# Gated delta rule: the triangular solve of a unit split over two pipeline steps, in straight code

## The reference

```python
q = l2norm(short_conv(h @ Wq)) * SCALE; k = l2norm(short_conv(h @ Wk)); v = short_conv(h @ Wv)   # conv of 4 taps, silu
g_eff = -exp(A_log) * softplus(h @ Wf1 @ Wf2 + dt_bias)      # 8 groups of 16 key channels
beta = sigmoid(h @ Wb)
def step(S, inp):
    qt, kt, vt, gt, bt = inp
    S = S * exp(gt)[..., None]
    err = einsum('bhk,bhkv->bhv', kt, S)
    delta = bt[..., None] * (vt - err)
    S = S + kt[..., None] * delta[:, :, None, :]
    return S, einsum('bhk,bhkv->bhv', qt, S)
y = o * silu(h @ Wg + bg)
y = y * rsqrt(mean(y * y, -1) + EPS) * norm_w
return y.reshape(B, T, H * DV) @ Wo
```

## Time and profile before

| | us |
|---|---|
| median of 3 runs | 6659.9 |
| profiled execution, its own time | 6661.47 |
| its span | 6659.7 |
| TensorE busy / weight loads | 6146.7 / 4309.7 |
| VectorE busy | 4830.9 |
| ScalarE busy | 2724.6 |
| GpSimd busy | 1811.1 |

### The profile page before, as it was taken

The page is one execution under the profiler, slowest core; times in us unless marked ns, Lnnn a source line. Parts: engine busy times, 40 slices in busy tenths (PEclk is TensorE's granted clock), DMA queues, the critical chain, the costliest instruction groups (busy, mean ns, idle before and its releaser), DMA issues. The chain is left out here.

```text
span 6659.7 us, 108024 instructions
## 1 busy us (share of the span) xinstructions
PE 6146.7 (92%) x33720; PEld 4309.7 (65%) x33720; DVE 4830.9 (73%) x7947; ACT 2724.6 (41%) x4746; POOL 1811.1 (27%) x1636
## 2 busy tenths in 40 slices
PE   5699999999999999999999999999999999899999
PEld 2467766766667667766777667766777777644444
DVE  7688878888788878887888788878888888611110
ACT  2344444444444444444444444444444444401101
POOL 2233333333333333333333333333333333200000
PEclk8899999999999999999999999999999999999999
DMA  2101010100010100101010101010100000032221
GB/s 71 43 25 30 21 33 26 32 25 27 26 32 26 27 25 25 32 25 30 22 33 25 33 25 29 22 33 26 32 26 27 25 26 26 16 114 81 85 78 43
DMA packets 183592, 234.20 MB, mean 35 GB/s; under 512 B 25048, under 2 KB 128088, under 8 KB 179168
## 3 DMA queue, kind: packets, MB, share of 16 engines
q1 hardware_dynamic: 111072, 188.22, 9.7%
q10 hardware_dynamic: 72192, 41.95, 2.2%
HBM read 183.75 MB, written 46.38 MB: 35 GB/s over the span
## 5 line engine op out<-in xcount | busy, mean ns | idle before, releaser
L659 PE MATMUL bank<-xT,weights 128*128 (+1 forms) x4096 | 2183.2, 631 | 87.3 <-DMA bg_col<-in_L_attn_bg 34.6
L1185 POOL TENSOR_TENSOR KR<-KR,decay_u 128x256 f32<-128x256 f32 x896 | 979.0, 1093 | 2358.1 <-PE bank L685 2358.1
L911 DVE TENSOR_TENSOR KQ<-KQ,decay_u 128x512 f32<-128x512 f32 x896 | 759.8, 848 | 602.2 <-PE bank L685 602.0
L685 PEld LDWEIGHTS bank<-KQ,KR 128*128 128x128 f32 x7168 | 919.2, 192 | 249.7 <-issue 216.3
L896 DVE SCALAR_TENSOR_TENSOR conv<-pre,taps,conv 128x512 f32<-128x512 f32 x1152 | 993.4, 862 | 27.3
L685 PE MATMUL bank<-KQ,KR 128*128 128x128 f32 x7168 | 954.7, 276 | 1.7 <-DVE KQ L911 1.7
L659 PEld LDWEIGHTS bank<-xT,weights 128*128 128x128 f32 x4096 | 660.6, 194 | 299.4 <-issue 216.8
L931 DVE COPY_PREDICATED all_pairs<-level_mask,bank 128x512 f32<-128x512 int32 x896 | 793.4, 885 | 0.0
L707 PEld LDWEIGHTS bank<-T_inv,pairs 128*128 128x128 f32 x3072 | 457.3, 193 | 470.3 <-issue 248.3
L707 PE MATMUL bank<-T_inv,pairs 128*128 128x64 f32 x3072 | 656.0, 339 | 62.0 <-DVE T_inv L947 59.6
L1103 ACT ACTIVATE T_inv<-bank 128x256 fp32r<-128x256 f32 x640 | 248.0, 388 | 792.6 <-PE bank L722 792.6
(11 more groups left out here) (162 smaller groups left out, 9129.5 us busy)
## 6 DMA issues: line engine op xcount, KB each, us to landing
decay_u<-decay_scratch SPq DMA_DIRECT2D x128, 510.0 KB
beta_u<-beta_scratch SPq DMA_DIRECT2D x128, 256.0 KB
y_scratch<-y_out ACTq DMA_DIRECT2D x128, 256.0 KB, 6.9
y_in<-y_scratch SPq DMA_DIRECT2D x32, 1024.0 KB, 4.8
xt<-in_L_attn_hidden_states SPq DMA_DIRECT2D x8, 1024.0 KB, 5.5
x_in<-in_L_attn_hidden_states SPq DMA_DIRECT2D x32, 256.0 KB, 5.0
out<-o_out ACTq DMA_DIRECT2D x32, 256.0 KB, 2.0
w<-in_L_ffn_W SPq DMA_DIRECT2D x8, 704.0 KB, 4.9
```

What stands on the lines that cost most here:

```text
L659: last = nc.tensor.matmul(bank[w % 2][:], weights[par][:, w, k, :], xT[:, k, bass.ds(j * UC, UC)], start=k == 0, stop=k == KC - 1)
L685: last = nc.tensor.matmul(to[:, :, i], KR[:, cols(i)], halves(KQ[:, :, cols(i)], l, 1), start=True, stop=True)
L911: nc.vector.tensor_tensor(second_halves, second_halves, pair[:, :, 0:1].unsqueeze(1).to_broadcast([P, 2, blocks, 1 << l]), ALU.mult).then_ ...
L1185: nc.gpsimd.tensor_tensor(first_halves, first_halves, second.to_broadcast([P, UC >> (l + 1), 1 << l]), ALU.mult).then_inc(keys_scaled.sem, 1)
```

## The change

- A fourth role: unit `c = a - 3`. The step of `b` ends with the first delta and the product of `refine(b, 0)`; both corrections, the second refinement, output and state, the gated output, its norm and the store are done for `c` in the next step, between the projections and the first levels. X, gate, k_rows, pairs_scan and chunk_decay have two buffers each. k_hat and q_hat now lie in silu, v_u in conv, y_out in y_rn, residual in U_r.
- Banks: T goes to bank 5 and X to bank 2 in the inverse; the solve has bank 7.
- v comes into bank 7 by four transposes (`is_transpose=True`), followed by the four products with the state; before, four fp32 products with the identity alternated with them.
- ScalarE's list: the copy KQ_scan (`keep_scaled`) now stands ahead of the table load and the two `inverse_norm`; the silu of the gate is followed by the copies of T and X, projection 0 comes behind them. GpSimd makes the first X after level 2 of the step before its use.
- `walk` and SP's list are Python loops: 131 steps written out, no hardware loop. DVE no longer waits ahead of y_out for the store; ScalarE does, ahead of the Ln.

```diff
+        for n in range(H * J + 3):
+            a, m, b, c = (u if 0 <= u < H * J else None for u in (n, n - 1, n - 2, n - 3))
...
+            step(Step(**f))
@@ SP
+        for u in range(1, H * J):
+            h, j = u // J, u % J
+            if j == 1 and 1 <= h < H - 1:
+                load_next(h, h % 2)
+            wait(sp, unit_ready, u - 1, 1)
+            if u >= 2:
+                wait(sp, keys_scaled, u - 2, LEVELS)
+                wait(sp, chunk_decay_ready, u - 2, 1)
+            load_unit(h, j, u % 2)
@@ TensorE
+            def right_side():
...
                 for i in range(B):
-                    nc.tensor.matmul(bank[7][:, cols(i)], v_u[:, cols(i)], ident[:], start=True, stop=False)
+                    nc.tensor.matmul(bank[7][:, cols(i)], v_u[:, cols(i)], ident[:], is_transpose=True, start=i == 0,
+                                     stop=False, skip_group_check=True)
+                for i in range(B):
                     last = nc.tensor.matmul(bank[7][:, cols(i)], KQ_scan[:, 0, cols(i)], state[:, cols(i)], start=False,
-                                            stop=True)
+                                            stop=True, skip_group_check=True)
...
+            def y_sums():
+                if c is None:
+                    return
                 if a is not None:
                     wait(pe, sums_taken, a, 2)
+                wait(pe, y_sq_ready, c, 1)
...
+            correct_by_residual(0)
+            project(0, (0, 1))
+            inverse_z(1)
+            diagonal()
+            level(0)
+            inverse_xt(1)
+            refine(c, 1)
+            project(0, (2,))
+            inverse_z(2)
+            project(0, (3,))
+            level(1)
+            inverse_xt(2)
+            correct_by_residual(1)
+            project(1, (0,))
+            inverse_z(3)
+            project(1, (1,))
+            level(2)
+            inverse_xt(3)
+            project(1, (2,))
+            output_and_state()
+            inverse_z(4)
+            project(1, (3,))
+            level(3)
+            inverse_xt(4)
+            project(2, (0,))
+            inverse_z(5)
+            project(2, (1,))
+            level(4)
+            inverse_xt(5)
+            project(2, (2,))
+            inverse_z(6)
+            right_side()
+            level(5)
+            inverse_xt(6)
+            project(2, (3,))
+            output_of_state()
+            first_delta()
+            sums(0)
+            project(3, (0,))
+            level(6)
+            refine(b, 0)
+            sums(1)
+            project(3, (1,))
+            transpose_keys()
+            project(3, (2,))
             transpose_pairs()
+            y_sums()
+            project(3, (3,))
@@ VectorE
             halo(a, s.a_first, m, qk_conv_steps, 2 * TAPS, slice(0, 2), qk_halo_ready)
             halo(m, s.m_first, b, v_conv_steps, TAPS, slice(2, 3), v_halo_ready)
+            correct_delta(0)
             add_identity_to_z(1)
             keep_diagonal()
             scale(0)
             keep_pairs(0)
+            take_residual(c, 1)
+            add_identity_to_z(2)
+            scale(1)
+            keep_pairs(1)
+            correct_delta(1)
+            add_identity_to_z(3)
+            scale(2)
+            keep_pairs(2)
+            convolve(0, range(2))
+            gated_output()
+            add_identity_to_z(4)
+            scale(3)
+            keep_pairs(3)
+            next_state()
+            convolve(0, range(2, TAPS))
+            add_identity_to_z(5)
+            scale(4)
+            keep_pairs(4)
+            convolve(1, range(2))
+            add_identity_to_z(6)
+            scale(5)
+            keep_pairs(5)
+            convolve(1, range(2, TAPS))
             scale(LEVELS - 1)
             keep_pairs(LEVELS - 1)
+            take_residual(b, 0)
+            convolve(2)
+            keep_chunk_decay()
             unit_inputs()
             first_inverse()
+            normalised_output()
@@ ScalarE
+            silu_gate()
+            take_t(1)
+            take_x(1)
+            silu_v()
+            take_projection(0)
+            take_t(2)
+            take_x(2)
+            take_t(3)
+            take_x(3)
+            take_projection(1)
+            take_t(4)
+            take_x(4)
+            square_output()
+            silu_squares(0)
+            take_t(5)
+            take_x(5)
+            take_right_side()
+            take_x(6)
+            take_projection(2)
+            take_delta()
+            silu_squares(1)
+            keep_scaled()
+            nc.scalar.preload_act_table_set("natural_log_exp_and_others")
+            inverse_norm(0)
+            inverse_norm(1)
+            keep_rows()
+            keep_all_pairs()
+            inverse_rms()
+            store_output()
@@ GpSimd
+        def first_x(u, before):
+            wait_apart(pool, pairs_ready.sem, pairs_ready.at(u, 2), pool_waits_passed)
+            if before is not None:
+                wait_apart(pool, correction_done.sem, correction_done.at(before, REFINEMENTS), pool_waits_passed)
+            nc.gpsimd.tensor_tensor(X[u % 2][:], pairs[:, 0], ident_each[:], ALU.add).then_inc(x1_ready.sem, 1)
...
             for l in range(LEVELS):
                 if l >= LEVELS - 2:
                     squares_left(s.a, l - (LEVELS - 2))
                 scale_keys(s.m, 1 - s.odd, l)
-
-            wait_apart(pool, t_done.sem, t_done.at(s.m, 1), pool_waits_passed)
-            nc.gpsimd.tensor_tensor(X[:], pairs[:, 0], ident_each[:], ALU.add).then_inc(x1_ready.sem, 1)
+                if l == 2:
+                    first_x(s.m, s.c)
```

More of the change, by code:

```diff
@@ L536, in walk @@
     def walk(eng, step):
[L539 to L563, removed]
+        for n in range(H * J + 3):
+            a, m, b, c = (u if 0 <= u < H * J else None for u in (n, n - 1, n - 2, n - 3))
+            f = dict(odd=n % 2, a=a, m=m, b=b, c=c)
+            if a is not None:
+                f.update(ja=a % J, par_a=a // J % 2, a_first=a % J == 0)
+            if m is not None:
+                f.update(jm=m % J, par_m=m // J % 2, m_first=m % J == 0)
+            if b is not None:
+                f.update(par_b=b // J % 2)
+            if c is not None:
+                f.update(h=c // J, j=c % J, ends=c % J == J - 1)
+            step(Step(**f))
     block = ctx.enter_context(nc.Block())
@@ L829, in step @@
-            correct_by_residual(1)
-            project(3, (3,))
-            if b is not None:
-                wait(pe, delta_refined, b, REFINEMENTS)
-                for i in range(B):
-                    last = nc.tensor.matmul(bank[6][:, cols(i)], delta[:, cols(i)], pairs_scan[:, 1, cols(i)], start=False,
-                                            stop=i == B - 1, skip_group_check=True)
+                wait(pe, u_kept, b, 1)
+                apply_inverse(b, U_r).then_inc(delta_done.sem, 1)
@@ new lines, in refine @@
+            def refine(u, n):
+                if u is None:
+                    return
+                if n == 0:
+                    wait(pe, pairs_kept, u, 1)
+                    wait(pe, delta_ready, u, 1)
+                else:
+                    wait(pe, delta_refined, u, n)
+                for i in range(B):
+                    last = nc.tensor.matmul(bank[7][:, cols(i)], pairs_scan[u % 2][:, 0, cols(i)], delta[:, cols(i)],
+                                            start=True, stop=True)
+                last.then_inc(product_done.sem, 1)
@@ new lines, in correct_by_residual, with output_and_state @@
+            def correct_by_residual(n):
+                if c is None:
+                    return
+                wait(pe, residual_ready, c, n + 1)
+                apply_inverse(c, residual).then_inc(correction_done.sem, 1)
+            def output_and_state():
+                if c is None:
+                    return
+                wait(pe, delta_refined, c, REFINEMENTS)
+                for i in range(B):
+                    last = nc.tensor.matmul(bank[6][:, cols(i)], delta[:, cols(i)], pairs_scan[c % 2][:, 1, cols(i)],
+                                            start=False, stop=i == B - 1, skip_group_check=True)
@@ new lines, in gated_output, with next_state @@
+            def gated_output():
+                if c is None:
+                    return
+                wait(dve, o_done, c, 1)
+                wait(dve, gate_ready, c, 1)
+                nc.vector.tensor_tensor(yg[:], bank[6][:], gate[c % 2][:], ALU.mult).then_inc(yg_ready.sem, 1)
+            def next_state():
+                if c is None:
+                    return
+                wait(dve, s_done, c, 1)
+                if s.ends:
+                    nc.vector.memset(state[:], 0.0).then_inc(state_ready.sem, 1)
+                else:
+                    wait(dve, chunk_decay_ready, c, 1)
+                    for i in range(B):
```

(3 more changed lines are left out.)

339 lines of the change are left out of this document (117 added, 222 removed).

## The result

The changed kernel takes 6688.0 us (median of 6 runs, 6686.3 to 6692.2) against 6657.5 us before (median of 6, 6652.5 to 6662.2). The ratio is 1.0047, with a 95% interval of 1.0034 to 1.0060: slower by 31 us, where 230 us less were forecast. The changes of layout came much as forecast, and with them one wait of 3.07 us in each step that was not in the sum, with a fall of TensorE's clock behind it in most steps.

The account below looks back on a forecast made before the run. TensorE was nearest to full before; afterwards the ring over VectorE and ScalarE sets the step. Step 26.0 + 15.75 = 41.75 us against 43.56, rounded to 230 us less: 6430 us, 8-in-10 range 6340 to 6620.

Parts of the forecast that it names:

- TensorE in the tail: End of step: sums(1) wait for GpSimd until +8.15, 1.2 us late; TensorE's queue reaches z(1) at +15.3, before T_inv.
- The four rivals: A: scale(6) late, 6600 us (0.20); B: TensorE bounds, 6315 (0.09); C: GpSimd's products, 6730 (0.12); D: loops' cost stays, 6515 (0.04).
- rival C: GpSimd's whole-tile products hold VectorE on the path: step 44.1 us, 68 us slower, 6730 us; chance 0.12.
- z(1) to level 5: From a unit's first inverse product, z(1), to the start of its level 5: 26.0 us.
- stop at xt(5): TensorE waits at xt(5) for VectorE's ZI(5), a new stop of 0.95 us that nothing hides.
- scale(6) starts, takes: VectorE's scale(6) starts at +6.14 after level 5, 0.23 us ahead of GpSimd's second product, and takes 0.69 us.
- T_inv: T_inv starts 3.15 us after k_hat in the tail, and z(1) follows 0.73 us later.
- z(1): Next step's first inverse product starts at +15.75 us after level 5, set by T_inv.
- The ring over VectorE and ScalarE: Tail path over VectorE and ScalarE sets the step; TensorE's queue is ready 0.4 us ahead of T_inv.
- v by transpose: Four transposes replace four fp32 products of v with the identity: saving at most 0.5, at least 0.3 us.
- No loops: Straight code runs every step like the last two heads: 42.91 us against 43.56, 0.65 us a step, 82 us in all.
- One more step: 131 steps for 130, the last holding only half a solve: counted 0, bounds -5 and +5 us.

Follow-up runs that it names:

- after: The changed kernel as measured, with the whole change applied to the kernel before: 6688.0 us, ratio 1.0047.
- the one with a bank of its own: Changed kernel with the second sums sent to bank 5 in place of bank 2, so they no longer wait for the first Ln: 6356.0 us, ratio 0.955.
- the old order: Kernel before with loops written out, and the copy to KQ_scan moved ahead of the table load and inverse norms: 6852.1 us, ratio 1.029.
- the kernel in which scale(6) misses its gap: Changed kernel with the KQ_scan copy behind both inverse norms, plus refine(b, 0) moved ahead of level 6: 6449.2 us, ratio 0.9687.

## Why the prediction was wrong

*The failed step is "TensorE in the tail".* It had sums(1) wait for GpSimd only and start at +8.15 us after level 5. The code of `sums` has a second wait, for the Ln that empties bank 2, and the diff moved that Ln behind the copy and the table load: it ended at +9.74, and the sums started at +9.88. I had both halves of it in the text (ScalarE's new order, with the Ln's times, and the sums' place in TensorE's queue) and did not lay one against the other. In the kernel before, the Ln came early and this wait ended no stop, so no view of before names it.

*Its price.* Against the kernel in which the sums do wait for GpSimd only (41.19 us a step), the wait costs 1.26 us a step, to 42.45, and the clock 1.65 us in 103 of 124 steps. Together 332 us. The clock is the second thing that the prediction had at nothing without a reason: no term of its sum and none of its rivals has it, though the trace of before shows it at the back-edges. The four rivals had no such mechanism; rival C was right in sign and wrong in cause, since scale(6) was not hit and no product held the path.

*Steps that held*, times from the start of level 5 or of z(1), in a step of after:

| step | forecast | measured |
|---|---|---|
| z(1) to level 5 | 26.0 | 25.95 (42.45 - 16.50 in the short step) |
| stop at xt(5) | 0.95 | 0.58 |
| scale(6) starts, takes | +6.14, 0.69 | +5.96, 0.69 |
| GpSimd's second product | +6.37 | +6.33 |
| copy, table load | 1.04, 1.28 | 1.06, 1.28 |
| k_hat | +11.85 | +12.01 (3332.58) |
| T_inv | +15.0 | +15.15 (3335.72) |
| z(1) | +15.75 | +18.17; +16.50 with the clock kept |

The ring over VectorE and ScalarE is thus where I had put it, and T_inv was on time. It was TensorE that came late, by the wait. One agreement is luck: the parts that I gave from z(1) to level 3 add up to 16.5 us, not to the 16.7 that I went on with; the changed kernel has 16.75 and the one with a bank of its own 16.46. The parts as they stand would have given a step of 41.55 us and some 6405 us.

*v by transpose*: 0.48 us a step where TensorE is the bound, 0.16 where it is not; forecast 0.3 to 0.5. *No loops*: 102 us, forecast 82; the looped steps away from an outer back-edge cost 0.4 us more each, not 0.2. *One more step*: the first y_sums comes 44.4 us later (355.54 against 311.11 of the earlier trace rows), one step, and 124 full distances follow in place of 125; so 125 steps compare with 125. From there to the end of the span are 899.0 us (6686.3 - 5787.3), where before there were 903.3 (6659.7 - 5756.4): 4 us less, inside the bounds of 5.

*The forecast of the kernel I had in mind* was 6430; that kernel takes 6356. The 74 us are 0.56 us a step: 0.35 between z(1) and level 5 (25.65 for 26.0), where the stop at xt(5) alone is 0.37 shorter, and 0.19 in the tail, where z(1) came at +15.56 in place of +15.75. T_inv releases z(1) there, as forecast (it ends at +15.50).

*Where the time of the change lies*, by the runs: straight code -102 us; v by transposes -22 to -55; to the 302 us between the kernel before and the one with a bank of its own 145 to 178 are missing. I put them down to the split of the solve, though the split alone wasn't run. They are what is left after the copy's new place, which costs 89 us even with the bank free (6356.0 against 6267.3), so the rest of the change must be worth more than they say. Then the wait +154 and the clock +178.

*Open*: why the clock falls in 103 steps and not in 21 with the same stop. The trace has a pattern: the fall starts 39.3 to 40.8 us after the y_sums product, in consecutive steps mostly 0.2 to 0.3 us later each time, and after it has come to 40.3 us or more one step has none and the row starts again. No run tests what makes it so.

## What to carry to other kernels

When an engine's queue is reordered, list from the code every wait that other engines have on what was moved, those that never showed in the trace too: such a wait can become the bound as soon as its releaser moves. A copy that nobody needs soon belongs behind the instruction that frees TensorE's next bank. Where TensorE must stand for a few us, look at its clock behind the stop, which here cost half as much again as the stop itself; three products that nobody reads, put into the stop, made this kernel 178 us faster.

## What the runs showed of the hardware

- After a stop of 3.07 us within a step of 44 us, in which TensorE had been busy, the granted clock fell to 1.2 GHz for some 3.4 us in 103 of 124 steps, at 1.65 us each. With 2.74 us of the gap filled and 0.50 left it fell in none.
- A shorter stop is no safeguard: in the old order, steps with stops of 1.00 and 1.42 us within 3.6 us had it fall in 76 of 125, at 1.9 to 2.6 us where no head ends. With the stop of 1.00 alone (the loops written out) it fell in none. Nor does the longest stop alone decide: the kernel in which scale(6) misses its gap has stops of 1.4 and 0.8 us, 8.6 us apart, and a mean granted clock of 0.987 over the execution, as the other kernels here whose steps are alike (after: 0.961).
- The hold between VectorE and GpSimd works both ways: scale(6) ahead of the product stays at 0.69 us and the product takes 1.46 in place of 1.27 (3326.53 and 3326.90 in after).
